# Three sums of a state-space layer's step size move from VectorE to GpSimd

## What is computed

```python
delta = jax.nn.softplus(dt + b_dt)
A = -jnp.exp(A_log)
def step(h, inp):
    dlt_t, B_t, C_t, x_t = inp
    dA = jnp.exp(dlt_t[:, :, None] * A)
    h = h * dA + dlt_t[:, :, None] * B_t[:, None, :] * x_t[:, :, None]
    y_t = jnp.einsum('bdn,bn->bd', h, C_t)
```

## Time and profile before

| what | value |
|---|---|
| three runs, median (lowest to highest) | 3141.8 us (3126.4 to 3141.92) |
| span of the profiled execution, first to last instruction | 3131.4 us |
| the profiled execution's own time | not listed apart from its span |
| busy in the span: PE, DVE, ACT, POOL | 78%, 66%, 51%, 54% |
| scan loop | about 1633 to 2751 us of the span |
| busy in that loop: DVE, POOL, ACT | 1091.8, 744.0, 689.6 of 1118 us |
| mean granted TensorE clock | 0.918 |

### The profile page before, as it was taken

One profiled execution on the slowest core, in us unless ns is written; L12 is line 12 of the kernel. 1 busy time (PEld: TensorE's weight loads), 2 busy tenths in 40 slices (PEclk: granted clock), 3 DMA queues, 4 the chain that ended last, 5 costly groups with the idle time before them and its releaser, 6 DMA issues. The chain is left out here.

```text
span 3131.4 us, 49074 instructions
## 1 busy us (share of the span) xinstructions
PE 2457.7 (78%) x12952; PEld 1742.2 (56%) x12952; DVE 2073.9 (66%) x6083; ACT 1589.5 (51%) x3093; POOL 1699.2 (54%) x1349
## 2 busy tenths in 40 slices
PE   4239996885799844399979888888888889769991
PEld 4239994664699733299933333333343334349991
DVE  6414445775444455155539999999999999955553
ACT  3115554773355443155545666666656666425550
POOL 5745550455355447555515566776666667645551
PEclk9999997996899976699989999999999999879996
DMA  9147771211677532477723344444433344337775
GB/s 330 53 129 229 225 228 59 68 52 42 197 229 227 158 109 72 123 227 226 228 83 129 129 135 141 141 137 137 137 128 130 136 136 144 104 115 228 226 228 171
DMA packets 268819, 479.26 MB, mean 153 GB/s; under 512 B 37453, under 2 KB 181803, under 8 KB 268560
## 3 DMA queue, kind: packets, MB, share of 16 engines
q1 hardware_dynamic: 225280, 405.41, 42.5%
q0 software_dynamic: 34816, 68.00, 6.1%
q10 hardware_dynamic: 8592, 4.33, 0.5%
HBM read 383.22 MB, written 98.54 MB: 154 GB/s over the span
## 5 line engine op out<-in xcount | busy, mean ns | idle before, releaser
L1736 POOL TENSOR_TENSOR ssm_HC<-ssm_H,ssm_BC 128x1024 f32<-128x1024 f32 x255 | 599.8, 2352 | 407.2 <-DVE ssm_psX L1806 338.3
L1492 PE MATMUL ssm_psY<-ssm_HC,ident 128*128 128x512 f32 x1020 | 517.4, 632 | 114.5 <-POOL ssm_HC L1736 114.3
L1650 ACT ACTIVATE ssm_dA<-ssm_delta,A 128x511 f32<-128x511 f32 x512 | 333.0, 710 | 189.1 <-DVE ssm_H L1815 119.9
L1492 PEld LDWEIGHTS ssm_psY<-ssm_HC,ident 128*128 128x128 f32 x1020 | 190.9, 197 | 382.1 <-POOL ssm_HC L1736 192.2
L1813 DVE TENSOR_TENSOR_SCAN ssm_H<-ssm_dA,ssm_psX 128x512 f32<-128x512 f32 x256 | 308.7, 1206 | 0.0
L1815 DVE TENSOR_TENSOR_SCAN ssm_H<-ssm_dA,ssm_psX 128x512 f32<-128x512 f32 x256 | 304.3, 1189 | 0.0
L471 POOL DMA_INDIRECT xslots<-att_r_xn,att_r_idx x128 | 128.3, 1002 | 178.5 <-DVE att_r_idx L451 140.4
L877 POOL DMA_INDIRECT a_back<-a_yr,a_to_row x144 | 139.8, 971 | 150.8 <-DVE a_yr L952 128.8
L877 POOL DMA_INDIRECT b_back<-b_yr,b_to_row x144 | 139.8, 971 | 150.6 <-DVE b_yr L952 128.6
L877 POOL DMA_INDIRECT d_back<-d_yr,d_to_row x144 | 139.8, 971 | 147.2 <-DVE d_yr L952 125.3
L877 POOL DMA_INDIRECT c_back<-c_yr,c_to_row x144 | 139.8, 971 | 144.7 <-DVE c_yr L952 121.0
(11 more groups left out here) (566 smaller groups left out, 5811.0 us busy)
## 6 DMA issues: line engine op xcount, KB each, us to landing
ssm_BC<-bc_rows SPq DMA_DIRECT2D x128, 1024.0 KB, 5.5
a_W<-in_l_pack SPq DMA_DIRECT2D x72, 514.0 KB, 3.4
b_W<-in_l_pack SPq DMA_DIRECT2D x72, 514.0 KB, 3.4
c_W<-in_l_pack SPq DMA_DIRECT2D x72, 514.0 KB, 3.4
d_W<-in_l_pack SPq DMA_DIRECT2D x72, 514.0 KB, 3.3
a_xs<-xslots SPq DMA_DIRECT2D x72, 131.0 KB
b_xs<-xslots SPq DMA_DIRECT2D x72, 131.0 KB
c_xs<-xslots SPq DMA_DIRECT2D x72, 131.0 KB
```

What stands on the lines that cost most here:

```text
L1492: last = nc.tensor.matmul(psY[:, dt, :], k.ident[:, :], HC[:, n % RP, dt, :], start=(n == 0), stop=(n == NB - 1))
L1650: last = nc.scalar.activation(dA[:, n % RA, dt, 1:], delta[:, b, dt, 1:], ACT.Exp, scale=A[:, dt, n:n + 1])
L1736: nc.gpsimd.tensor_tensor(HC[:, n % RP, :, :], H[:, n % RH, :, :], BC[:, n // CHUNK % SLOTS, 1, n % CHUNK:n % CHUNK + 1, :].to_broadcast([ ...
```

## The change

- `correct`, `lengthen` and the sum of delta go from VectorE's queue to GpSimd's, behind HC of the states 12, 13 and 14 (for the first sequence: ahead of the loop). `weigh` on VectorE keeps ux and waits for `delta_ready`.
- GpSimd gets `rest - 1` ready made: ScalarE has one more activation of 128x1024 in `soften`, with a semaphore of its own (`less_ready`).
- The eight scatters of a router turn are issued as four behind HC of the states 8 to 11 and four behind HC of the states 0 to 3 of the next sequence. In the last sequence they stay as they were.
- In `Norm`, `Router.dve_0` and `Router.dve_2c`, for all stages, five short instructions with one source (`tensor_scalar`, `tensor_copy`) become ones with two, the second a row of zeros, ones, eps or eps squared that the load stage fills. The halving of the mean (line 211) goes; the factors where the mean is used are halved instead.

```diff
--- before.py
+++ after.py
@@ -208,12 +208,11 @@
...
         yield from chain.link(nc.vector.tensor_tensor(o, st[:, :, 1], st[:, :, 4], ALU.subtract))
-        nc.vector.tensor_scalar(m, m, 0.5, None, ALU.mult)
         yield from chain.link(nc.vector.scalar_tensor_tensor(out=o, in0=o, scalar=0.25, in1=o, op0=ALU.mult, op1=ALU.mult))
         yield from chain.link(nc.vector.scalar_tensor_tensor(out=v, in0=v, scalar=1.0 / D, in1=o, op0=ALU.mult, op1=ALU.add))
-        last = nc.vector.tensor_scalar(w[:, 0, :], v, EPS, None, ALU.add)
+        last = nc.vector.tensor_tensor(w[:, 0, :], v, self.k.eps[:, 0:T], ALU.add)
         if self.w == 2:
-            last = nc.vector.tensor_scalar(w[:, 1, :], v, 1.0 + EPS, EPS * EPS, ALU.mult, ALU.add)
+            last = nc.vector.scalar_tensor_tensor(out=w[:, 1, :], in0=v, scalar=1.0 + EPS, in1=self.k.eps_eps[:, 0:T], op0=ALU.mult, op1=ALU.add)
         last.then_inc(self.asked, 1)
@@ -236,7 +235,7 @@
...
         T = self.cut(s)[1]
-        return nc.vector.scalar_tensor_tensor(out=self.shift[:, 0:T], in0=self.mean[:, 0:T], scalar=-1.0, in1=self.rstd[:, self.w - 1, 0:T], op0=ALU.mult, op1=ALU.mult)
+        return nc.vector.scalar_tensor_tensor(out=self.shift[:, 0:T], in0=self.mean[:, 0:T], scalar=-0.5, in1=self.rstd[:, self.w - 1, 0:T], op0=ALU.mult, op1=ALU.mult)
 
@@ -339,11 +338,11 @@
...
         if not self.first:
-            yield from chain.link(nc.vector.scalar_tensor_tensor(out=n.back[:, 0:T], in0=n.mean[:, 0:T], scalar=-0.5, in1=n.rstd[:, 0, 0:T], op0=ALU.mult, op1=ALU.mult))
-            last = nc.vector.tensor_scalar(n.rstd[:, 0, 0:T], n.rstd[:, 0, 0:T], 0.5, 1.0, ALU.mult, ALU.add)
+            yield from chain.link(nc.vector.scalar_tensor_tensor(out=n.back[:, 0:T], in0=n.mean[:, 0:T], scalar=-0.25, in1=n.rstd[:, 0, 0:T], op0=ALU.mult, op1=ALU.mult))
+            last = nc.vector.scalar_tensor_tensor(out=n.rstd[:, 0, 0:T], in0=n.rstd[:, 0, 0:T], scalar=0.5, in1=k.ones_row[:, 0:T], op0=ALU.mult, op1=ALU.add)
         last.then_inc(n.scaled, 1)
         self.free(dve, b, turn)
-        nc.vector.tensor_scalar(self.rows(s, b)[:, :, D], k.token[:, bass.ds(t0, T)], 1.0, None, ALU.mult)
+        nc.vector.tensor_tensor(self.rows(s, b)[:, :, D], k.token[:, bass.ds(t0, T)], k.zeros[:, 0:T], ALU.add)
 
@@ -448,7 +447,7 @@
...
         yield from chain.link(nc.vector.tensor_reduce(row, pos.rearrange("p t (c e) -> p t c e", c=TOPK), AX.X, ALU.add))
-        nc.vector.tensor_copy(self.ids(s, b), row.rearrange("p t c -> p (t c)")).then_inc(self.rowed, 1)
+        nc.vector.tensor_tensor(self.ids(s, b), row.rearrange("p t c -> p (t c)"), k.zeros[:, 0:TOPK * T], ALU.add).then_inc(self.rowed, 1)
 
@@ -798,6 +797,8 @@
...
             nc.vector.memset(k.ones[:, :], 1.0)
+            for row, value in ((k.zeros, 0.0), (k.ones_row, 1.0), (k.eps, EPS), (k.eps_eps, EPS * EPS)):
+                nc.vector.memset(row[:, :], value)
             clear_rows(nc, empty[:, :]).then_inc(cleared, 1)
@@ -1356,8 +1357,8 @@
...
             sem, "linked setup closed normed flipped turned fronted emptied z_fronted z_done silu_done mixes mixed".split())
-        projected, low_ready, one_ready, dt_summed, v_half, v_ready, abs_ready, u_ready, l_ready, rest_ready, sized, delta_ready, ux_ready = map(
-            sem, "projected low_ready one_ready dt_summed v_half v_ready abs_ready u_ready l_ready rest_ready sized delta_ready ux_ready".split())
+        projected, low_ready, one_ready, less_ready, dt_summed, v_half, v_ready, abs_ready, u_ready, l_ready, rest_ready, sized, delta_ready, ux_ready = map(
+            sem, "projected low_ready one_ready less_ready dt_summed v_half v_ready abs_ready u_ready l_ready rest_ready sized delta_ready ux_ready".split())
         dA_ready, dBx_half, dBx_done, h_half, h_ready, hc_ready, y_summed, y_ready, out_summed, added, cleared = map(
@@ -1635,6 +1636,8 @@
...
                 nc.scalar.activation(rest[:, :, :], soft, ACT.Identity, bias=1.0).then_inc(one_ready, 1)
+                act.wait_ge(one_ready, s + 1)
+                nc.scalar.activation(rest[:, :, :], rest[:, :, :], ACT.Copy, bias=-1.0).then_inc(less_ready, 1)
 
@@ -1727,15 +1730,44 @@
...
         def _(pool):
+            def correct(s):
+
+                pool.wait_ge(less_ready, s + 1)
+                nc.gpsimd.tensor_tensor(rest[:, :, :], soft, rest[:, :, :], ALU.subtract).then_inc(rest_ready, 1)
+
+            def lengthen(s):
+                pool.wait_ge(l_ready, s + 1)
+                pool.wait_ge(rest_ready, s + 1)
+                nc.gpsimd.tensor_tensor(rest[:, :, :], absv, rest[:, :, :], ALU.add).then_inc(sized, 1)
+
+            def sum_up(s, b):
+                pool.wait_ge(sized, s + 1)
+                pool.wait_ge(v_ready, s + 1)
+                nc.gpsimd.tensor_tensor(delta[:, b, :, :], rest[:, :, :], v[:, :, :], ALU.add).then_inc(delta_ready, 1)
+
             R.pool_start(pool)
+            correct(0)
+            lengthen(0)
+            sum_up(0, 0)
             for s in range(BATCH):
-                for n in range(NB if s < LAST else NB - 1):
+                b, after = s % 2, there(s + 1)
+                for n in range(NB if after else NB - 1):
                     pool.wait_ge(h_ready, s * NB + n + 1)
...
                     nc.gpsimd.tensor_tensor(HC[:, n % RP, :, :], H[:, n % RH, :, :], BC[:, n // CHUNK % SLOTS, 1, n % CHUNK:n % CHUNK + 1, :].to_broadcast([P, DT, SEQ]), ALU.mult).then_inc(hc_ready, 1)
-                    if n >= 8 and there(s - 2):
-                        R.pool_one(pool, s - 2, s % 2, n - 8)
+                    if n < 4 and there(s - 3):
+                        R.pool_one(pool, s - 3, 1 - b, n + 4)
+                    if 8 <= n < 12 and there(s - 2):
+                        R.pool_one(pool, s - 2, b, n - 8)
+                    if n >= 12 and not after:
+                        R.pool_one(pool, s - 2, b, n - 8)
+                    if n == 12 and after:
+                        correct(s + 1)
+                    if n == 13 and after:
+                        lengthen(s + 1)
+                    if n == 14 and after:
+                        sum_up(s + 1, 1 - b)
             R.pool_one(pool, LAST - 2, 1, 7)
@@ -1753,20 +1785,7 @@
...
 
-            def correct(s):
-
-                dve.wait_ge(one_ready, s + 1)
-                nc.vector.scalar_tensor_tensor(out=rest[:, :, :], in0=rest[:, :, :], scalar=-1.0, in1=soft, op0=ALU.add, op1=ALU.subtract, reverse1=True).then_inc(rest_ready, 1)
-
-            def lengthen(s):
-                dve.wait_ge(l_ready, s + 1)
-                dve.wait_ge(rest_ready, s + 1)
-                nc.vector.tensor_tensor(rest[:, :, :], absv, rest[:, :, :], ALU.add).then_inc(sized, 1)
-
             def weigh(s, b):
-                dve.wait_ge(sized, s + 1)
-                dve.wait_ge(v_ready, s + 1)
-                nc.vector.tensor_tensor(delta[:, b, :, :], rest[:, :, :], v[:, :, :], ALU.add).then_inc(delta_ready, 1)
                 dve.wait_ge(delta_ready, s + 1)
@@ -1823,8 +1842,6 @@
...
             straight(N.dve_stats(nc, chain, 1), normalize(1))
-            correct(0)
-            lengthen(0)
             weigh(0, 0)
@@ -1847,10 +1864,6 @@
...
                         small.begin(R.dve_2a(nc, dve, chain, s - 1, 1 - b))
-                    if n == 13 and after:
-                        correct(s + 1)
-                    if n == 14 and after:
-                        lengthen(s + 1)
                     if n == (13 if after else 11) and before:
@@ -1884,6 +1897,7 @@
...
         k.token, k.slot = sb("token", [P, TILES]), sb("slot", [P, SPREAD])
+        k.zeros, k.ones_row, k.eps, k.eps_eps = (sb(n, [P, 4 * SEQ_TILES]) for n in ("zeros", "ones_row", "eps", "eps_eps"))
         k.pad_row = sb("pad_row", [P, EXPERTS], I32)
...
         k.block_row = sb("block_row", [P, NBLK], I32)
```

## The result

The changed kernel takes 3153.2 us (median of six runs, 3150.2 to 3154.93), the kernel before 3136.0 us (six runs, 3126.4 to 3141.92). The ratio is 1.0057, 95% interval 1.0038 to 1.0075: slower, by 17 us and not by the 37 us of the forecast. The profiled execution took 3152.97 us with a span of 3151.2, 19.8 us over the 3131.4 of before.

What follows compares the result with a forecast made beforehand. VectorE, 98% busy, was taken to bound the scan loop. Turns 31.9 + start 3.5 - small instructions 2 + clock 4 = 37.4 us, on the median 3141.8: 3179 us, 1.2% slower; range 3150 to 3198.

Steps and rivals of the forecast that it cites:

- the sum of the turns: The 15 passages from one sequence to the next in the scan loop: 31.9 us slower in all.
- part 3: Sums on GpSimd at each turn: its queue, 2.35 us per instruction plus 0.1, delays ux by 2.13 us.
- the two late turns: Two of 14 turns where ScalarE was already late: ux 2.48 us later in each.
- part 6: TensorE idles 5.2 us at the turn instead of 3.8, greater clock falls come oftener: 0 to 8 us, taken as 4.
- Part 1: VectorE gives up the three sums: 4.2 us per turn, 63 us over 15 turns, if nothing replaced them.
- Part 2: ScalarE's extra pass ends line 407 1.09 us later; line 417 starts 0.31 us later, 1.09 in two turns.
- The start: First sequence's sums ahead of the loop, with the extra pass: ux starts 3.5 us later.
- Part 4: Scatters moved to states 0 to 3 are hidden, cost 0; left where they were, about 2 us longer path.
- Part 5: Small VectorE instructions: line 211 gone saves 2 us; second sources 0, with -4.4 us kept as a bound.
- (a): Rival: same chain, worse, with lower clock every turn and half-way, 2.48 us turns, second stop: 3190 to 3200, chance 0.12.
- (b): Rival: wait of ux does not bind, saved VectorE time shows, needing sums of 1.28 us: 3111, chance 0.11.
- (c): Rival: chain holds but next states take it back, VectorE's early waits for TensorE shrinking: 3162, chance 0.10.

Runs made afterwards that it cites:

- e4_early: Changed kernel with the router's exponential (line 407) ahead of the logarithm on ScalarE; 3152.95 us, ratio 1.0071.
- e11_nopass: Changed kernel without ScalarE's extra pass, GpSimd's first sum replaced by a product of the same size (no longer computes the layer); 3153.43 us, ratio 1.0048.
- e12_fill: Kernel before with matmuls of zeros in TensorE's idle times, 4 at the turn, 1 and 2 half-way; 3114.98 us, ratio 0.9928.
- e3_unsplit: Changed kernel with all eight scatters behind HC of states 8 to 15, as before; 3198.46 us, ratio 1.0214.
- e1_small: Kernel before with the edits of the small VectorE instructions alone (second source, line 211 gone); 3134.56 us, ratio 1.0009.
- e6_ahead: Changed kernel with GpSimd's sums one state earlier, line 407 ahead of the logarithm, scatters split five and three; 3117.83 us, ratio 0.9937.
- e15_pass_fill: Kernel before with ScalarE's extra pass alone plus matmuls of zeros on TensorE (4 at the turn, 1 and 2 half-way); 3122.2 us, ratio 0.9958.
- e9_fill: Kernel before with eight matmuls of zeros on TensorE at the turn; 3153.17 us, ratio 1.0052.
- e16_room_fill: Changed kernel with sums a state earlier, router's choice behind ux, its places a state later, plus 1, 1 and 2 matmuls of zeros; 3099.81 us, ratio 0.9888.

## Why the prediction was right or wrong

Direction and mechanism were right, the size twice too large: 37.4 us forecast, 17.2 measured on the medians and 19.8 on the two profiled spans. The term that failed is the sum of the turns, 31.9 us said and 19.5 measured: in part 3 the step from one GpSimd instruction to the next was taken too long (2.45 us for 2.31), and the two late turns were priced as if they stayed. A second term, part 6's 4 us for the clock, was 0.6. Step by step:

- **Part 1** (4.2 us a turn given up): VectorE's busy time in the loop fell by 45 us where 63 was said. The held lines 418 (0.17 us more) and 421 (1.13 more) make up 18 us in 14 turns; nothing hung on it, since VectorE waits in the end.
- **Part 2** (line 407 later by 1.09 us): right to 0.02 us, 0.72 to 1.81 us after the scan. But its cost to line 417 is inside the turn that GpSimd sets (e4_early, e11_nopass), as the chain in part 3 had it.
- **Part 3, the turn**: the chain is right link by link, and the mis-sized term is the step between two instructions of GpSimd. I added 0.1 us to their length of 2.35. In a queue without waits they follow each other every 2.31 us (2266.18, 2268.49, 2270.80), 0.04 less than one lasts. That is 0.14 us at each of four links, and the fifth, from the first sum's end over lines 418 and 1806 to HC of state 13, took 0.80 us instead of 0.93: 0.7 us a turn, 12.93 us instead of 13.62. In 11 turns 7.6 us, and 0.4 in the turn after sequence 1, which came 1.76 us later instead of 2.13.
- **Part 3, the late turns**: forecast at 2 x 2.48 us more. They are gone, so that their two turns grew by 0.5 us only: 4.0 us. The prediction took the late line 407 for a property of the turn. It is the trace of a fall of the clock half-way, which did not come in the changed kernel.
- The first turn cost 0.9 us instead of 1.4. All turns together: 19.5 us (19.4 from the unrounded rows), forecast 31.9. The prediction's "some 6 us less" at 2.25 us a sum comes out as 4.7 for its 47 sums on the path; nothing hangs on it.
- **The start**: 2.13 us later, forecast 3.5. From the logarithm's end to ux it is 1630.15 to 1635.14, 4.99 us, against 2.52; that and the pass make 3.56, so the chain held. What ran ahead of it was 1.4 us earlier in this execution, as executions of the same code up to there differ (first product at 1634.28 in before, 1632.28 in e12_fill).
- **Part 4** (scatters free where they were put): no start or middle grew, and e3_unsplit shows what they would cost on the path, 3.7 us a turn and not 2. The prediction left out the one ahead of the first sum.
- **Part 5**: line 211 went as said; at full clock the start is 0.14 us shorter a sequence, the 2 us of the forecast. The middle grew by 0.1 us (by 0.08 in e1_small), which was not foreseen and takes back 1.3 us. The bound of -4.4 us was none: the two stops are as long as before.
- **Part 6, the clock**: right that the greater fall would come nearly always (TensorE idles 4.97 us at the turn, 5.2 said), wrong that this costs 4 us. Starts are 24.69 us against 24.63: the fall also starts earlier and lies more in the idle time. Measured against full clock the difference is 12 x 0.05 = 0.6 us.
- **The base**: I put a sum made on the profiled execution on the median of three runs. That execution's time, if it has the 1.8 us beside its span that the one of after has, was 3133.2, well below 3141.8. That is 8.6 us of the 26 by which 3179 missed. Span against span the forecast was 17.6 too high: 12.4 in the turns, 1.4 at the start of the loop, 3.7 in the starts of the sequences (line 211 and the clock, +2 said, -1.7 measured) and 1.4 in what follows the loop, less the 1.3 of the middles.

Of the rivals, (a) needed falls half-way and turns of 2.48 us, which did not come; (b) needed a sum of 1.28 us, and it was 2.35; (c), that later states take it back, was nearest in time (3162) but not in kind: the wait of the earlier trace rows is 0.66 us instead of 1.17, by the place of the fall, but over the sequences 2 to 13 VectorE's waits for TensorE in the first 26 us did not shrink (1.17 us a sequence, 1.02 before).

## What to carry to other kernels

Before you move work from the bounding engine to a slower one, follow the last consumer's chain through the slower engine's queue from start to start, and put the moved work where nobody bound by that chain stands behind it: the same three sums cost 17 us behind states 12 to 14 and gained 36 behind 11 to 13 with the router's choice out of the way, of which 15 are left against a kernel before whose clock is kept full. If a kernel has runs spread over half a per cent, look at the granted clock in slices of 1 us over its inner loop; short idle times of TensorE that recur may be worth filling, if the filler is smaller than the gap (0.7% here with all gaps filled, a loss with one overfilled, and nothing where no one waits for TensorE). Make the sum against the time of the profiled execution, and forecast a difference, not a level.

## What the runs showed that was not expected

- A VectorE instruction of 128x32 with two sources in SBUF stood for up to 2.32 us beside one wide sum of GpSimd (e4_early) and ended within 0.1 us of its end. Beside two GpSimd instructions in close order it took the seam between them in every turn of the changed kernel (line 421, 1.31 us), but stood through the second as well in 11 turns of e6_ahead (line 418, 3.34 us) and in 13 of e3_unsplit (line 421, 4.85 us). What decides was not found.
- GpSimd instructions over 128x1024 f32 follow each other every 2.30 to 2.32 us in a queue without waits, with records of 2.34 to 2.36 us.
- Costs of the clock do not add up: ScalarE's pass cost 19 us alone, 5 us at full clock (7 by the medians of e15_pass_fill and e12_fill, taken on different chips) and none inside the change. What decided was whether TensorE's work that VectorE waits for fell under the lower clock, and that shifts with tenths of a microsecond in the order of the work.
- Keeping the clock up at the turn alone, with filler longer than the gap, went with falls half-way in 8 sequences of 12 instead of 2 (e9_fill); filler that fits, at the turn alone, was not tried. What makes TensorE's clock fall in one sequence of before and not in the next was not settled; only that, with the gaps filled, it did not fall in sequences 1 to 13 of the two kernels, while in e16_room_fill it still fell.
